# Node stage of a graph kernel: the stores of the per-block sums leave SyncE's queue and are issued by ScalarE, each behind its own copy

## Chip, cores and metric

The kernel runs on one core of one Trainium2 chip. The metric is the device time of one launch in microseconds (us); lower is better. Engine names: PE is TensorE, PEld its weight loads, DVE is VectorE, ACT is ScalarE, POOL is GpSimd, SP is SyncE. SPq and ACTq are the instruction sequencers of SP and ACT where they issue DMAs.

## What is computed

The reference is one layer of a graph network with a residual. `x` is 50000 x 128 in fp32, and there are 12500 edges.

```python
h = jnp.maximum(_layernorm(x, axis=-1), 0.0)
xx = _resmlp(h, w1[0], b1[0], w2[0], b2[0], wout[0])     # for every node
xs, xp, xd = (_resmlp(h, ... [m])[dst] for m in (1, 2, 3))
s = xx + segment_sum(gs * xs, src, n)
p = segment_sum(gp * xp[:, None, :], src, n)
d = segment_sum(gd * xd[:, None, :], src, n)
y = s + (pa * pb).sum(-2) + (da * db).sum(-2)
out = x + _resmlp(y, w1[4], b1[4], w2[4], b2[4], wout[4])
```

`_resmlp(x)` is `silu(x + silu(silu(x) @ w1 + b1) @ w2 + b2) @ wout`. `gs`, `gp`, `gd` come from the edge attributes; `pa`, `pb`, `da`, `db` are the halves of `p` and `d` times two matrices.

## The kernel before

The launch has three stages, and each of the five engines runs its own list of instructions through all of them; semaphores tie the lists together. The node stage (`first_stage`) ends some 410 us into the span, the edge stage (`edge_phase`) at about 880 us, and the final stage (`final_stage`) is the rest. The change lies in the node stage alone.

The nodes are cut into NB = 98 blocks of 512 rows; a block is a 128 x 512 tile, 256 KB. The node stage does two things at once. It normalises every block into `h` and stores it to the table `node_h` (`htab`), and for the first NA = 90 blocks it runs MLP 0 to the end and stores the result to `node_sums` (`ysum`). Beside this the edges are sorted in two passes by DVE (`picked`), PE (L859) and POOL's scatters (L506); POOL's `keep_pace` ties the scatters to PE's progress.

The work is pipelined by a counter k, written out by hand without a loop on the chip. In step k PE does four things in this order:

- the transpose of block k (L871), which waits for the normalised block from ACT (`nrm_a`) and DVE (`nrm_v`)
- the first matmul of block k-1 (L884), which waits for ACT's silu `s1`
- the second matmul of block k-2 (L891), which waits for `s2`
- the third of block k-3 (L899, into the bank `BANK_O`), which waits for `s3` and, by `row_done`, for the copy that empties that bank.

In two steps of five the seven bf16 matmuls of the sort (L859) stand between L871 and L884.

In step k ACT does, in this order:

- silu `s1` of block k (L798)
- part of the normalisation of block k+1 (L784; in most steps two tiles of 128 x 128, in some four, with DVE doing the rest at L626 and L635), one of them here and one behind L808
- silu `s2` of block k-1 (L808)
- silu `s3` of block k-2 (L817)
- the copy of block k-3 from the bank to `rowout` (L823), which raises `row_done`.

`rowout` has four slots, so the copy of block b also waits until the store of block b-4 has landed (`stored`). The copy is the last thing of a step.

SP's list in step k is: store of `h` of block k (`store_h`, L410), store of the sums of block k-4 (`store`, L400, which waits for `row_done`), load of the rows of block k+18 (`load_x`, L392; `xin` has 20 slots). Steps 12 to 19 also store zeros (L460). SP runs strictly in this order.

In the final stage ACT issues the stores of the output already (L1103), but there the row is made by DVE (L1054), and the store belongs to the block of four steps back.

Of the kernel before, what the change touches and what calls it, by code (L numbers as in the profile page):

```python
# [78 lines left out]
def gnn_kernel(nc, x, src, dst, attr3, attr32, attr5, w_rs, w_rp, w_rd, w_pp, w_pd,  # L79
# [15 lines left out]
    NB = -(-N // BLOCK)  # L95
    ND = 8
    FILL = 4
    NA = NB - ND
# [35 lines left out]
    with ctx:  # L134
# [48 lines left out]
        rowout = sb("rowout", [P, 4, TB, F])  # L183
# [51 lines left out]
        at = P * T  # L235
# [39 lines left out]
        def at(b):  # L275
            return slice(N - BLOCK, N) if b == NB - 1 else slice(b * BLOCK, (b + 1) * BLOCK)

        def first_stage():
# [106 lines left out]
            def sync(sp):  # L385
                def load_x(b):
                    s = b % NX
                    if b >= NX:
                        if by_vector(b - NX + 1):
                            sp.wait_ge(nrm_v, by_vector(b - NX + 1))  # L390
                        sp.wait_ge(nrm_a, b - NX + 1)
                    sp.dma_start(xin[:, s, :, :], xb_view(at(b), x)).then_inc(x_in[s], 16)  # L392

                def store(b):
                    s = b % 4
                    sp.wait_ge(row_done, b + 1)
                    if b == NB - 1:

                        sp.wait_ge(stored[(b - 1) % 4], 16 * ((b - 1) // 4 + 1))
                    sp.dma_start(xb_view(at(b), ysum), rowout[:, s, :, :]).then_inc(stored[s], 16)  # L400

                def store_h(b):
                    s = b % 4
                    sp.wait_ge(nrm_a, b + 1)
                    if by_scalar(b) < TB:
                        sp.wait_ge(nrm_v, by_vector(b + 1))
                    if b == NB - 1:

                        sp.wait_ge(h_stored[(b - 1) % 4], 16 * ((b - 1) // 4 + 1))
                    sp.dma_start(xb_view(at(b), htab), xn[:, s, :, :]).then_inc(h_stored[s], 16)  # L410

                load_x(0)
                load_x(1)
                sp.wait_ge(s_staged, 1)
                assert load_parts(src, st_src[:, :], sp, s_src, 1) == N_SRC
                load_x(2)
                load_x(3)
                sp.dma_start(w1_sb[:, m, :], w1[m, :, :]).then_inc(s_w, 16)
                with nc.allow_non_contiguous_dma(reason="biases to partitions"):
                    sp.dma_start(b1_sb[:, :], b1.rearrange("m k -> k m"), allow_slow_non_contiguous=True).then_inc(s_w, 16)  # L420
                    sp.dma_start(b2_sb[:, :], b2.rearrange("m k -> k m"), allow_slow_non_contiguous=True).then_inc(s_w, 16)
                sp.dma_start(w2_sb[:, m, :], w2[m, :, :]).then_inc(s_w, 16)
                sp.dma_start(wo_sb[:, m, :], wout[m, :, :]).then_inc(s_w, 16)
                for b in range(4, 8):
                    load_x(b)
                sp.wait_ge(s_staged, 2)
                n_rest = 0
                for dram, tile, per in ((dst, st_dst, 1), (attr3, st3, NP3), (attr5, st5, ND5), (attr32, st32, NRBF)):
                    flat = tile[:, :] if per == 1 else tile[:, :, :].rearrange("p t c -> p (t c)")
                    n_rest += load_parts(dram, flat, sp, s_edges, per)  # L430
                assert n_rest == N_REST
                for b in range(8, NX):
                    load_x(b)
                store_h(0)
                store_h(1)
                for k in range(2, NB + 4):
                    if k < NB:
                        store_h(k)
                    if k == 6:
                        sp.wait_ge(s_cst, 5)  # L440
                        sp.dma_start(w1_sb[:, m + 1:, :], w1[m + 1:, :, :].rearrange("m k n -> k m n")).then_inc(s_w2, 16)
                        sp.dma_start(w2_sb[:, m + 1:, :], w2[m + 1:, :, :].rearrange("m k n -> k m n")).then_inc(s_w2, 16)
                        sp.dma_start(wo_sb[:, m + 1:, :], wout[m + 1:, :, :].rearrange("m k n -> k m n")).then_inc(s_w2, 16)
                        sp.dma_start(wpp_sb[:, :], w_pp).then_inc(s_w2, 16)
                        sp.dma_start(wpd_sb[:, :], w_pd).then_inc(s_w2, 16)
                        for j in range(TB):
                            for n, w in enumerate((w_rp, w_rd, w_rs)):
                                sp.dma_start(wr_sb[j * Q:j * Q + NRBF, n, :], w).then_inc(s_w2, 16)
                    if k == 10:
                        for row, parts, each in groups:  # L450
                            sp.dma_start(by_src[row:row + parts * each, :].rearrange("(p t) w -> p t w", t=each),
                                         padrow[0:parts, 0:each, :]).then_inc(s_init, 16)
                        for lo in range(0, SPARE, TB):
                            n = min(TB, SPARE - lo)
                            sp.dma_start(ysum[N + lo * P:N + (lo + n) * P, :].rearrange("(t p) f -> p t f", p=P),
                                         zeros[:, 0:n * F].rearrange("p (t f) -> p t f", t=n)).then_inc(s_init, 16)
                    if 12 <= k < 12 + ND:
                        lo = (NA + k - 12) * BLOCK
                        hi = min(lo + BLOCK, N)
                        sp.dma_start(ysum[lo:hi, :].rearrange("(p t) f -> p t f", t=TB),  # L460
                                     zeros[0:(hi - lo) // TB, :].rearrange("p (t f) -> p t f", t=TB)).then_inc(s_init, 16)
                    if 0 <= k - 4 < NA:
                        store(k - 4)
                    if NX <= k + NX - 2 < NB:
                        load_x(k + NX - 2)
                for s in s_scat:
                    sp.wait_ge(s, 2 * 16 * CHUNKS)
                sp.wait_ge(s_init, 16 * (-(-SPARE // TB) + len(groups) + ND))
                with nc.allow_non_contiguous_dma(reason="one word of each row"):
                    for g in (0, 1):  # L470
                        load_group(sp, by_src, er, rq, nxt, g, g, TB, T, rows_in[g], rows_in[g] if g else first_index_in)
# [301 lines left out]
            def scalar(act):  # L773
# [19 lines left out]
                for k in range(NB + 3):  # L793
                    if k < NK:
                        act.wait_ge(xT_done, k + 1)
                        if k >= 3:
                            act.wait_ge(a_done, k - 2)
                        nc.scalar.activation(s1[:, k % 3, :], BANK_X[k % 4][:, :], ACT.Silu).then_inc(s1_done, 1)  # L798
                    norm(k + 1, 0)
                    norm(k + 1, 1)  # L800
                    norm(k + 1, 2)
                    if 0 <= k - 1 < NK:
                        act.wait_ge(a_done, k)
                        if k == 1:
                            act.wait_ge(s_w, 16 * 5)
                        if k >= 4:
                            act.wait_ge(b_done, k - 3)
                        nc.scalar.activation(s2[:, (k - 1) % 3, :], BANK_A[:, :], ACT.Silu, bias=b1_sb[:, m:m + 1]).then_inc(s2_done, 1)  # L808
                    norm(k + 1, 3)
                    if 0 <= k - 2 < NK:  # L810
                        act.wait_ge(b_done, k - 1)
                        if k - 2 >= NA:
                            act.wait_ge(nrm_v, by_vector(NB - NB % NX + 4 + FILL))
                        elif k >= 5:
                            act.wait_ge(o_done, k - 4)
                        target = s3[:, (k - 2) % 3, :] if k - 2 < NA else kept_rows(k - 2 - NA)
                        nc.scalar.activation(target, BANK_X[(k - 2) % 4][:, :], ACT.Silu, bias=b2_sb[:, m:m + 1]).then_inc(s3_done, 1)  # L817
                    if 0 <= k - 3 < NA:
                        b = k - 3
                        act.wait_ge(o_done, b + 1)  # L820
                        if b >= 4:
                            act.wait_ge(stored[b % 4], 16 * (b // 4))
                        nc.scalar.copy(rowout[:, b % 4, :, :].rearrange("p t f -> p (t f)"), BANK_O[:, :]).then_inc(row_done, 1)  # L823

            def tensor(pe):
                start = dict(stop=True, skip_group_check=True)
# [1191 lines left out]
```

## Time and profile before

| what | value |
|---|---|
| median of 3 runs | 1187.74 us (1185.68 to 1198.05) |
| the profiled execution's own time | 1187.62 us |
| its span, first to last instruction | 1185.8 us |
| around the span | 1.8 us |
| busy over the span: PE, DVE, ACT, POOL | 92%, 58%, 62%, 40% |
| mean granted TensorE clock | 0.977 of full |

"Span" is the time from the first to the last instruction of the profiled execution; its own time is that plus the 1.8 us around it. "Busy" counts an engine's own work. Register, branch, semaphore and DMA-issuing instructions are not counted as busy, so SP has no busy time at all, and what ACT spends on issuing a DMA does not show in ACT's share either. In a timeline the bracket behind a row tells how long the engine was idle before it and what ended that.

### The profile page before, as it was taken

To read this page: it belongs to the slowest core of one execution; us is meant where nothing else is said; L and a number is where in the kernel's file an instruction comes from. 1 tells how busy PE (TensorE), PEld (TensorE's weight loads), DVE (VectorE), ACT (ScalarE), POOL (GpSimd) and SP (SyncE) were. 2 spreads that over 40 slices of the span, in tenths; PEclk is the share of its full clock that TensorE was granted. 3 is DMA by queue.
4 is the path that set the end of the run, shared out by engine and by line. 5 is a ranking of instruction groups with operands and counts; after the bars stand their busy time and mean duration, and the time that the engine had idled before them with its cause. 6 is when DMAs were issued, how large, how long until landed. Compare 5 with 4: busy or idle time off the path is not lost.

```text
span 1185.8 us, 22908 instructions
## 1 busy us (share of the span) xinstructions
PE 1088.6 (92%) x6267; PEld 711.7 (60%) x6267; DVE 688.9 (58%) x2413; ACT 736.6 (62%) x1379; POOL 471.7 (40%) x433
## 2 busy tenths in 40 slices
PE   4978998987898659999999999999979999999998
PEld 2645665765666326666666666666736666666665
DVE  8976776766666226656665665655633444444432
ACT  4656878966778635665565565555536666666664
POOL 2355666155666442556556656655440000000000
PEclk9988999999999879999999999999999999999999
DMA  9667767855674443665556555555549999999984
GB/s 267 208 201 232 225 223 222 296 170 175 224 228 155 142 94 75 115 118 107 97 102 107 99 95 106 101 96 92 101 69 240 282 268 274 274 271 273 269 275 142
DMA packets 319187, 210.81 MB, mean 178 GB/s; under 512 B 204084, under 2 KB 240830, under 8 KB 318963
## 3 DMA queue, kind: packets, MB, share of 16 engines
q1 hardware_dynamic: 280770, 164.67, 50.7%
q0 software_dynamic: 24208, 19.29, 10.3%
q10 hardware_dynamic: 14112, 25.70, 6.2%
q8 instruction: 44, 0.72, 0.3%
q14 instruction: 53, 0.43, 0.1%
HBM read 107.15 MB, written 102.42 MB: 177 GB/s over the span
## 4 chain that ended last, share of the span: by engine, by line
PE 83%; DVE 6%; issue 5%; ACT 2%; another core or an unknown queue 2%; DMA 2%; POOL 0%; SPq 0%; ACTq 0%; POOLq 0%; DVEq 0%
PE quad L1133 8%; PE bank L1147 7%; PE bank L1769 6%; PE quad L884 5%; PE quad L1139 5%; PE bank L1779 5%; PE bank L899 5%; PE bank L1845 4%; PE quad L891 4%; PE bank L1815 4%; PE bank L1846 3%; PE quad L871 3%; PE quad L1855 2%; PE quad L1122 2%
## 5 line engine op out<-in xcount | busy, mean ns | idle before, releaser
L1421 POOL DMA_INDIRECT node_sums<-rowout,row_i x98 | 154.8, 1580 | 49.6 <-issue 28.7
L74 POOL DMA_INDIRECT yin<-node_h,er x98 | 99.2, 1012 | 165.1 <-DMA nxt<-edges_by_src 130.9
L1054 DVE TENSOR_TENSOR rowout<-bank,xin 128x512 f32<-128x512 f32 x98 | 67.8, 692 | 142.7 <-PE bank L1147 141.7
L1147 PEld LDWEIGHTS bank<-wo_sb,s 128*128 128x128 f32 x784 | 102.8, 191 | 47.8 <-issue 47.8
L899 PEld LDWEIGHTS bank<-wo_sb,s 128*128 128x128 f32 x720 | 95.3, 194 | 54.6 <-issue 54.5
L506 POOL DMA_INDIRECT edges_by_low<-pay,rank_i x98 | 99.7, 1017 | 69.5 <-issue 28.9
L1473 DVE SCALAR_TENSOR_TENSOR h<-bank,b_sb,hT 128x512 f32<-128x512 f32 (+1 forms) x75 | 55.5, 740 | 123.3 <-PE bank L1779 113.6
L506 POOL DMA_INDIRECT edges_by_src<-pay,rank_i x98 | 98.9, 1009 | 60.8 <-issue 24.4
L784 ACT ACTIVATE xn<-xin,nbias,rnorm 128x128 f32<-128x128 f32 x222 | 106.4, 493 | 13.0 <-DVE nbias L616 10.5
L681 DVE SCALAR_TENSOR_TENSOR picked<-bank,onehot 128x256 bf16<-128x256 f32 (+1 forms) x196 | 67.5, 387 | 74.1 <-PE bank L859 29.6
L1133 PE MATMUL quad<-s,w_sb 128*128 128x512 f32 x196 | 103.8, 612 | 0.8 <-ACT s L1071 0.7
L1147 PE MATMUL bank<-wo_sb,s 128*128 128x128 f32 x784 | 103.5, 275 | 0.9 <-DVE rowout L1054 0.9
L899 PE MATMUL bank<-wo_sb,s 128*128 128x128 f32 x720 | 96.9, 278 | 7.9 <-ACT rowout L823 5.7
L884 PE MATMUL quad<-s,w_sb 128*128 128x512 f32 x188 | 101.8, 625 | 0.1
L565 DVE BATCH_NORM_STATS2 stat<-xin 128x6 f32<-128x128 f32 x392 | 98.6, 283 | 1.1 <-DMA xin<-in_x_dram 1.1
L1652 ACT ACTIVATE s<-h 128x512 f32<-128x512 f32 (+1 forms) x75 | 46.6, 622 | 72.7 <-DVE h L1473 56.6
L1681 ACT COPY AB<-bank 128x512 f32<-128x512 f32 x98 | 58.1, 593 | 54.1 <-PE bank L1846 41.9
L1769 PE MATMUL bank<-s,w_sb 128*128 128x512 f32 (+1 forms) x150 | 79.9, 615 | 6.9 <-ACT s L1644 4.8
L871 PE MATMUL quad<-ident,xn 128*128 128x128 f32 x284 | 45.5, 284 | 38.7 <-issue 21.0
L808 ACT ACTIVATE s<-quad,b_sb 128x512 f32<-128x512 f32 x94 | 64.6, 687 | 21.4 <-PE quad L884 11.9
L1779 PE MATMUL bank<-s,w_sb 128*128 128x512 f32 (+1 forms) x150 | 76.2, 590 | 0.1
L891 PE MATMUL quad<-s,w_sb 128*128 128x512 f32 x142 | 75.7, 616 | 0.0
(208 smaller groups left out, 2254.4 us busy)
## 6 DMA issues: line engine op xcount, KB each, us to landing
xin<-in_x_dram SPq DMA_DIRECT2D x196, 256.0 KB
node_h<-xn SPq DMA_DIRECT2D x98, 256.0 KB
out_dram<-rowout ACTq DMA_DIRECT2D x98, 256.0 KB
node_sums<-rowout SPq DMA_DIRECT2D x90, 256.0 KB
yin<-node_sums SPq DMA_DIRECT2D x53, 256.0 KB, 3.7
yin<-node_sums SPq DMA_DIRECT2D x180, 64.0 KB, 3.2
src_in_every_row<-edge_src_row SPq DMA_DIRECT2D x24, 256.0 KB
border_sums_by_tile<-border_sums SPq DMA_DIRECT2D x24, 256.0 KB, 2.1
```

The source lines that it names most:

```text
L74: pool.indirect_dma_start(out=xg[:, s, j, :], out_offset=None, in_=x, in_offset=bass.IndirectOffsetOnAxis(ap=er[:, s, j, 1:2].bitcast(mybi ...
L506: nc.gpsimd.indirect_dma_start(out=ps.dram, out_offset=bass.IndirectOffsetOnAxis(ap=rank_i[:, t:t + 1], axis=0), in_=pay[:, t, :], in_offs ...
L565: last = nc.vector.bn_stats(stat[:, b % 32, j, :], xin[:, s, j, :])
L784: ins = nc.scalar.activation(xn[:, b % 4, j, :], xin[:, s, j, :], ACT.Relu, bias=nbias[:, q, i:i + 1], scale=rnorm[:, q, i:i + 1])
L884: nc.tensor.matmul(BANK_A[:, :], w1_sb[:, m, :], s1[:, (k - 1) % 3, :], start=True, stop=True).then_inc(a_done, 1)
L891: nc.tensor.matmul(BANK_X[(k - 2) % 4][:, :], w2_sb[:, m, :], s2[:, (k - 2) % 3, :], start=False, stop=True, skip_group_check=True).then_i ...
L899: last = nc.tensor.matmul(BANK_O[:, j * P:(j + 1) * P], s3[:, (k - 3) % 3, j * P:(j + 1) * P], wo_sb[:, m, :], start=True, stop=True)
L1133: nc.tensor.matmul(BANK_A[:, :], w1_sb[:, m, :], s1[:, s, :], start=True, stop=True).then_inc(a_done, 1)
L1147: last = nc.tensor.matmul(BANK_O[:, j * P:(j + 1) * P], s3[:, s, j * P:(j + 1) * P], wo_sb[:, m, :], start=True, stop=True)
L1421: nc.gpsimd.indirect_dma_start(out=ysum, out_offset=bass.IndirectOffsetOnAxis(ap=row_i[:, t % 2, j:j + 1], axis=0), in_=urow[:, t % 2, j, ...
L1769: nc.tensor.matmul(BANK_A[:, 0:e], w1_sb[:, MLP[m], :], s1[:, k % 2, 0:e], start=True, stop=True).then_inc(a_done, 1)
L1779: nc.tensor.matmul(BANK_B[:, 0:e], w2_sb[:, MLP[m], :], s2[:, m, 0:e], start=True, stop=True).then_inc(b_done, 1)
```

## The change

The store of a block's sums is taken out of SP's list. ACT issues it directly behind its copy of the same block, after a wait on `row_done` for that copy's own end. SP keeps the stores of `h`, the zeros and the loads. Everything else is the same; the branch for the last block falls away, since block NB-1 was never among the NA blocks stored here.

```diff
@@ def sync(sp) @@
-                def store(b):
-                    s = b % 4
-                    sp.wait_ge(row_done, b + 1)
-                    if b == NB - 1:
-
-                        sp.wait_ge(stored[(b - 1) % 4], 16 * ((b - 1) // 4 + 1))
-                    sp.dma_start(xb_view(at(b), ysum), rowout[:, s, :, :]).then_inc(stored[s], 16)
@@
-                    if 0 <= k - 4 < NA:
-                        store(k - 4)
                     if NX <= k + NX - 2 < NB:
                         load_x(k + NX - 2)
@@ def scalar(act) @@
                         nc.scalar.copy(rowout[:, b % 4, :, :].rearrange("p t f -> p (t f)"), BANK_O[:, :]).then_inc(row_done, 1)
+                        act.wait_ge(row_done, b + 1)
+                        act.dma_start(xb_view(at(b), ysum), rowout[:, b % 4, :, :]).then_inc(stored[b % 4], 16)
```

ACT's list of the kernel before, from the copy at the end of one step through the next step (a step with two normalisation tiles), with the semaphores that each row waits for; `rowout` is the tile that is stored, `xn` the normalised block, `s` the silus:

```order
L823 COPY rowout<-bank 128x512 [waits n_o_done]
L798 ACTIVATE s<-quad 128x512 [waits n_a_done,n_xT_done]
L784 ACTIVATE xn<-xin,nbias,rnorm 128x128 [waits h_stored3,n_xT_done,n_norm_steps_done]
L808 ACTIVATE s<-quad,b_sb 128x512 [waits n_b_done,n_a_done]
L784 ACTIVATE xn<-xin,nbias,rnorm 128x128 [waits n_xT_done,n_norm_steps_done]
L817 ACTIVATE s<-quad,b_sb 128x512 [waits n_o_done,n_b_done]
```

The changed kernel's list there, beginning with the rest of that step; all lines of ACT stand ten lower, L813 is the copy:

```order
L774 ACTIVATE xn<-xin,nbias,rnorm 128x128 [waits h_stored3,n_xT_done,n_norm_steps_done]
L798 ACTIVATE s<-quad,b_sb 128x512 [waits n_b_done,n_a_done]
L774 ACTIVATE xn<-xin,nbias,rnorm 128x128 [waits n_xT_done,n_norm_steps_done]
L807 ACTIVATE s<-quad,b_sb 128x512 [waits n_o_done,n_b_done]
L813 COPY rowout<-bank 128x512 [waits n_o_done]
L815 DMA node_sums<-rowout 128x512 [waits n_row_done]
L788 ACTIVATE s<-bank 128x512 [waits n_a_done,n_xT_done]
L774 ACTIVATE xn<-xin,nbias,rnorm 128x128 [waits h_stored0,n_xT_done,n_norm_steps_done]
```

One row came in, L815, between the copy and the next step's first silu. It waits for `n_row_done`, which the copy just ahead of it raises. There are 90 such rows.

SP's list of the kernel before, around the last store of zeros (`node_h` is the table of `h`, `node_sums` the sums, `xin` the rows of `x`):

```order
L410 DMA node_h<-xn 128x512 [waits n_rectified_by_vector,n_rectified_by_scalar]
L460 DMA node_sums<-zeros 84x512
L400 DMA node_sums<-rowout 128x512 [waits n_row_done]
L392 DMA xin<-in_x_dram 128x512 [waits n_rectified_by_scalar,n_rectified_by_vector]
L410 DMA node_h<-xn 128x512 [waits n_rectified_by_vector,n_rectified_by_scalar]
L400 DMA node_sums<-rowout 128x512 [waits n_row_done]
```

The changed kernel's list at the same place:

```order
L402 DMA node_h<-xn 128x512 [waits n_rectified_by_vector,n_rectified_by_scalar]
L452 DMA node_sums<-zeros 84x512
L392 DMA xin<-in_x_dram 128x512 [waits n_rectified_by_scalar,n_rectified_by_vector]
L402 DMA node_h<-xn 128x512 [waits n_rectified_by_vector,n_rectified_by_scalar]
L392 DMA xin<-in_x_dram 128x512 [waits n_rectified_by_scalar,n_rectified_by_vector]
```

The row L400 with its wait is gone, 90 times, and the load of `x` follows the store of `h` directly.

## Rows read from the trace of the kernel before

**Rows 1.** Busy time by stretch of the node stage; x is the number of instructions.

```profile
core 0: us, PE busy (x) PEld busy (x) DVE busy (x) ACT busy (x) POOL busy (x), PEclk, DMA share, GB/s
60.00:120.00 60.00, 48.62 (x229) 32.29 (x228) 40.61 (x240) 37.37 (x73) 32.82 (x33) 0.86 0.66 216
...
180.00:240.00 60.00, 56.84 (x334) 39.54 (x332) 43.30 (x221) 51.02 (x105) 23.19 (x24) 1.00 0.76 258
...
sum 368.00, PE 323.46 PEld 221.38 DVE 254.82 ACT 274.71 POOL 207.63; mean PE 46.21 PEld 31.63 DVE 36.40 ACT 39.24 POOL 29.66
```

**Rows 2.** Chain of waits, 34 to 402 us, shares by line.

```profile
by line: PE quad L884 16.5%; PE bank L899 16.3%; PE quad L891 12.3%; issue 10.9%; PE quad L871 7.7%; DVE picked L681 4.5%; another core or an unknown queue 4.5%; PE bank L859 4.3%; PE bank L891 3.5%; DVE stat L565 3.5%; PE bank L834 3.3%; P
```

**Rows 3.** Timeline, 157 to 165 us: start us, us, engine, line, operation.

```profile
156.73 0.61 PE L871 MATMUL bank<-ident,xn 128*128 128x128 f32 x4
...
157.09 0.58 ACT L823 COPY rowout<-bank 128x512 f32<-128x512 f32 x1
157.55 0.61 ACT L798 ACTIVATE s<-bank 128x512 f32<-128x512 f32 x1
157.69 0.34 SPq L400 DMA_DIRECT2D node_sums<-rowout  x1
...
158.99 0.51 ACT L784 ACTIVATE xn<-xin,nbias,rnorm 128x128 f32<-128x128 f32 x1
159.38 0.71 ACT L817 ACTIVATE s<-quad,b_sb 128x512 f32<-128x512 f32 x1
...
159.79 0.60 PE L871 MATMUL quad<-ident,xn 128*128 128x128 f32 x4
...
162.02 0.58 ACT L823 COPY rowout<-bank 128x512 f32<-128x512 f32 x1 [1.94 <-remote]
162.17 0.42 DVE L681 SCALAR_TENSOR_TENSOR picked<-bank,onehot 128x256 bf16<-128x256 f32 x1 [0.95 <-PE bank L859]
...
163.95 0.49 ACT L784 ACTIVATE xn<-xin,nbias,rnorm 128x128 f32<-128x128 f32 x1
...
164.54 0.63 PE L871 MATMUL quad<-ident,xn 128*128 128x128 f32 x4 [0.66 <-issue]
```

**Rows 4.** Timeline of ACT: first and last copy with a short step behind it.

```profile
40.90 0.58 ACT L823 COPY rowout<-bank 128x512 f32<-128x512 f32 x1 [0.42 <-PE bank L899]
...
398.73 0.59 ACT L823 COPY rowout<-bank 128x512 f32<-128x512 f32 x1
...
401.64 0.58 ACT L823 COPY rowout<-bank 128x512 f32<-128x512 f32 x1
```

**Rows 5.** Waits on PE and DVE, 34 to 402 us: us in total, times, longest.

```profile
PE quad L871 <- issue: 21.0, 24, 2.4
PE bank L871 <- issue: 13.0, 6, 3.9
...
DVE xn L626 <- DMA node_h<-xn: 13.1, 7, 2.5
```

**Rows 6.** ACT's copy L823 in the whole run: durations, and waits before it.

```profile
L823 ACT COPY rowout<-bank x90: 567/585/601, 33.9 to 401.6; 128x512 f32<-128x512 f32 x90
...
  remote: 22.0, 12
```

**Rows 7.** Waits of SP's queue, 34 to 402 us: us in total, times, longest.

```profile
SPq L410 <- ACT xn L784: 88.6, 57, 4.4
SPq L400 <- ACT rowout L823: 39.1, 31, 5.3
```

**Rows 8.** Stores issued by ACT in the final stage, and one of them in the timeline.

```profile
L1103 ACTq DMA_DIRECT2D out_dram<-rowout x98: 338/344/1093, 899.4 to 1183.3; - x98
...
1006.52 0.36 ACTq L1103 DMA_DIRECT2D out_dram<-rowout  x1
1006.54 0.62 ACT L1088 ACTIVATE s<-xn 128x512 f32<-128x512 f32 x1
1007.06 0.59 ACT L1071 ACTIVATE s<-quad 128x512 f32<-128x512 f32 x1
```

## The prediction, made before the changed kernel ran

> **What bounds the kernel now.** I read the node stage alone, since no instruction of the two later stages moves, and began with busy time by stretch. Over the 368 us from the first copy to the last, PE works 323.5 us and ACT 274.7 us; in the densest stretch, 180 to 240 us, PE is at 57 of 60 and ACT at 51 of 60 [rows 1]. So PE sets the pace, and ACT is close behind. The chain of waits says the same: the largest shares are PE's matmuls L884, L899 and L891, and 10.9% stands under "issue", where the profile names nobody [rows 2].
>
> The timeline tells who that nobody is. At 164.54 us PE begins the transpose L871 after 0.66 us of idle time put down to "issue". ACT's last normalisation tile began at 163.95 and took 0.49, so it ended at 164.44, and PE started 0.10 us behind it [rows 3]. L871 does wait for that tile. There are 30 such waits before L871 in the stage, 34.0 us together [rows 5], and in 29 steps of 89 PE starts L871 after an idle time of over 0.3 us just 0.10 us behind the end of an ACT tile. At those places PE stands still until ACT has come through its list. In that list the copy L823 is ahead of the silu and the tiles.
>
> The rhythm: a copy at 157.09, the next silu already at 157.55, while the copy still runs until 157.67. The engine takes the next instruction 0.46 us after the start of the copy [rows 3]. With nothing in its way ACT needs 2.9 us from copy to copy (398.73 to 401.64) [rows 4]; PE needs 3.06 (L871 at 156.73 and at 159.79) [rows 3], and some 0.8 more in the two steps of five that hold the sort's matmuls. On the average a step takes 367.7 / 89 = 4.13 us, as there are stalls besides.
>
> **What the change removes.** SP loses 90 issues of 0.34 us and the wait for the copy, 39.1 us in 31 pieces [rows 7]. Behind that wait stood the load of `x` for 18 blocks further on, and then the store of the next `h`. In the ACT and PE waits of this stretch no load of `x` is named. The store of `h` waits for ACT's tiles anyway (88.6 us in 57 waits [rows 7]), and those come after the copy in ACT's order. I cost the removal at 0. If that is wrong, it is a gain; see the rivals.
>
> **What it adds.** 90 times ACT now holds its list until its own copy is done, and then issues a DMA. No row of before shows this pair on ACT, so I put it together:
>
> - the copy runs to its end: 0.585 us (median of 90) [rows 6]
> - the semaphore: the copy at 157.09 ended at 157.67, and SP's store began at 157.69, so 0.02 [rows 3]
> - the issue: ACT's own stores in the final stage take 0.34 [rows 8]
> - until the next instruction starts: PE follows ACT by 0.10 at 164.54 [rows 3]; I take 0.10.
>
> Sum 1.05 us from the start of the copy to the next silu, in place of 0.46: 0.59, rounded to **0.6 us per block**. The low end is 0.48, with nothing between the issue and the silu. The high end is 0.69: in the final stage a silu starts at 1007.06, 0.18 us after an issue that ran from 1006.52 to 1006.88 [rows 8], so 0.58 + 0.02 + 0.36 + 0.18 = 1.14 to 1.15, less 0.46. That row shows too why stores cost ACT nothing today: L1088 starts at 1006.54, while the issue runs. There the sequencer has sent the silu ahead and issues beside it. Here it can't, since the wait is for the instruction just sent.
>
> The Trainium skill (DMA: Bandwidth & Descriptors, Issuing engines are not separate DMA queues) says that issuing from several engines saves only sequencer time, which is usually small beside the transfer. By that rule SP saves 90 issues that nobody waits for, and the sum is not changed by a faster transfer.
>
> **How much of 90 x 0.6 = 54 us reaches the end.** ACT has 368.0 - 274.7 = 93.3 us of idle time in the stretch [rows 1], so both ends are open: all hidden, or all paid. I went through ACT's timeline from copy to copy. In 33 of the 89 steps ACT idles less than 0.3 us, in 8 more less than 0.6; the first of these 41 follows the copy at 40.90, the last the one at 398.73 [rows 4]. In the other 48 it waits 0.6 us or more for PE, and the addition hides there. Summing 0.6 less the idle time over the 41 gives 19.8 us (15.1 with 0.48, 23.6 with 0.69).
>
> That takes each lag of ACT as a lag of PE. In a step with no idle time PE has a little room: the tile at 158.99 ends at 159.50, and L871 starts at 159.79 [rows 3], 0.29 us later, so 0.19 to 0.3 may slip. If ACT may always lag 0.3 us before PE feels it, and the lag is carried from step to step and worked off in idle time, the same list gives 13.1 us (8.5 with 0.48, 16.6 with 0.69). But behind a stall there is no room: at 162.02 to 164.54 ACT has no idle time and PE waits for it. I take **15 us**, nearer to 13.1, since most short steps don't follow each other.
>
> After the last copy, at 401.64, nothing is added. The lag stays to the end, because the scatters keep PE's pace and the edge stage begins when both are done. Sum, against the profiled execution's own 1187.62 us: 1187.6 + 15 = 1202.6. The median of the runs, 1187.74, is the same within 0.1 us, so the forecast for the median is **1202.7 us**, 1.3% slower. Its own range runs from 8.5 to 23.6 us, 1196 to 1211.
>
> **Rivals.**
>
> *No difference.* ACT may lag further than I think before PE feels it. The copy only has to be done before the next L899, the last matmul of PE's step, and the silus are each wanted later than the tiles. With room for 1.2 us the list gives 2.9 us, 1190.6. Against it stand the 29 starts of L871 right behind an ACT tile.
>
> *Faster.* Before the copy stand 22.0 us in 12 waits put down to "remote" [rows 6]; the copy also waits for the landing of the store four blocks back, which shares SP's queue with 256 KB loads and 256 KB stores of `h`. DVE waits 13.1 us for the landing of `h` in 7 cases [rows 5]. If these are landings held up in SP's queue, a second queue shortens them. All of the 22.0 less the 15 that ACT pays would be 1187.6 - 7 = 1180.6; with ACT's cost hidden too, 1165.6. Against it: at 162.02 the copy is released, and at 162.17 DVE's `picked`, which waits for PE and for no store [rows 3]; so both were held by PE. In its favour is a rule of the Trainium skill (the same page, Queues, rings and completion order): each DMA engine goes round its queues packet by packet, so that a store in a queue of its own would not wait behind loads. Worked out from this kernel's rows that is the case just priced, at 1180.6, and no row before shows a store overtaking. As DVE runs ahead of ACT by design (it centres block k+1 in step k), I give its 13.1 us no worth.
>
> *Much slower.* The longer ACT step can cost PE more than the sum says, if nothing is worked off in the idle time: the stalls are waits in a ring ACT to PE to ACT, and then each of the 90 additions is paid. That is 54 us, 1241.6. It decides if the 48 long steps each become longer by 0.6. PE's clock may join: in 60 to 120 us, with PE busy 48.6 of 60, it was granted 0.86 [rows 1].
>
> **How the numbers follow.** The forecast (ACT's lag paid in the short steps, 8.5 to 24 us): 0.66. No difference, below 8.5 us: 0.22. Faster: 0.06. Much slower, 24 us and more: 0.06. A measurement of this kernel tells about 1%, 11.9 us, from no change. Within the forecast about four parts in five lie above 11.9 us, 0.53, and with the much slower case that makes 0.59 for slower by over 1%. The rest of the forecast, 0.13, with the 0.22 and a part 0.01 of the faster case makes 0.36 within 1%, and 0.05 is faster by over 1%. The range for 8 in 10 takes in the forecast's own and most of the case of no difference: 1189 to 1213.
>
> **What the changed profile would show.** ACTq issues of `node_sums`, 90 of 0.34 us, each within 0.05 us of the end of a copy, and the silu behind them 1.05 us after the start of the copy in place of 0.46. The shortest copy to copy at 3.5 us in place of 2.9. ACT's busy time unchanged, and the last copy at about 417 us in place of 401.6. More idle time before L871 on PE than 34 us. SP's wait on the copy gone and no other in its place. The later stages as long as before. I would be wrong if the silu followed the copy in 0.5 us (the issue is hidden after all), if the last copy came at 402 (all absorbed), or if the "remote" waits before the copy went away, for then they were landings.

## The result, and the profile after

The change made the kernel slower by 0.69%. Over 20 runs of each the median is 1197.62 us (1190.12 to 1204.13) against 1188.95 us (1182.84 to 1198.05) before; the ratio is 1.0069, 95% interval 1.0049 to 1.0088, which is 8.2 us (5.8 to 10.5) on 1188.95. (The two medians themselves lie 8.7 us apart.) By the bound of about 1% that the prediction names, that is within what counts as "same"; the interval leaves no doubt about the sign. The profiled execution has a span of 1196.9 us, 11.1 more than before.

The busy time of the changed kernel, for the same stretches and with the same columns as [rows 1]:

```profile
60.00:120.00 60.00, 47.16 (x233) 31.32 (x234) 42.26 (x248) 38.03 (x75) 32.94 (x34) 0.94 0.69 216
...
180.00:240.00 60.00, 54.95 (x308) 37.33 (x307) 44.02 (x225) 49.35 (x101) 23.65 (x26) 1.00 0.78 251
...
sum 368.00, PE 319.78 PEld 217.16 DVE 252.83 ACT 272.46 POOL 201.71; mean PE 45.68 PEld 31.02 DVE 36.12 ACT 38.92 POOL 28.82
```

The loss shows in the densest stretch: PE does 308 matmuls in 180 to 240 us where it did 334, and works 55.0 us instead of 56.8. ACT, too, has less busy time there. Over the whole 368 us PE works 319.8 us instead of 323.5. An engine that is held back by its own list does not look busier; it does less in the same time.

ACT's timeline of the changed kernel, which answers to [rows 3]:

```profile
150.73 0.58 ACT L813 COPY rowout<-bank 128x512 f32<-128x512 f32 x1 [1.43 <-remote]
151.35 0.34 ACTq L815 DMA_DIRECT2D node_sums<-rowout  x1
151.79 0.60 ACT L788 ACTIVATE s<-quad 128x512 f32<-128x512 f32 x1 [0.47 <-ACT rowout L813]
...
153.62 0.68 ACT L807 ACTIVATE s<-bank,b_sb 128x512 f32<-128x512 f32 x1
154.19 0.58 ACT L813 COPY rowout<-bank 128x512 f32<-128x512 f32 x1
```

The silu starts 1.06 us after the start of the copy; it was 0.46 to 0.48. The bracket says that ACT was idle for 0.47 us before the silu and puts that down to ACT's own copy. The copy ended before these 0.47 us began, at 151.31 us; the issue, which does not count as busy, fills 0.34 of them. From copy to copy the step takes 3.46 us, where ACT's shortest was 2.9 [rows 4]. 39 of the 89 steps now take 3.44 to 3.46 us, and none is shorter.

The copy in the whole run of the changed kernel, to be read beside [rows 6]; the waits of PE from 34 to 415 us and of SP's queue from 34 to 409 us, the last copy, beside [rows 5] and [rows 7]; and the stores of the final stage, beside [rows 8]:

```profile
L813 ACT COPY rowout<-bank x90: 568/585/591, 34.3 to 408.7; 128x512 f32<-128x512 f32 x90
...
  remote: 23.8, 13
...
  ACT s L788: 19.3, 41
```

```profile
PE quad L863 <- issue: 23.1, 43, 2.4
...
PE bank L891 <- ACT rowout L813: 10.3, 5, 4.5
PE bank L863 <- issue: 10.2, 14, 3.0
```

```profile
SPq L402 <- ACT xn L774: 105.8, 33, 7.4
```

```profile
L1095 ACTq DMA_DIRECT2D out_dram<-rowout x98: 338/354/393, 910.5 to 1194.4; - x98
```

The copies span 408.7 - 34.3 = 374.4 us against 367.7, so 6.7 of the 11.1 us by which this execution is longer lie between the first and the last copy. Another 0.4 us lie before the first copy, and 4.0 between the last copy and the first store of the final stage (910.5 - 408.7 against 899.4 - 401.6). The final stage's stores take 283.9 us in both. The transpose L863 (L871 before) has 57 waits put down to "issue", 33.3 us in all, instead of 30 with 34.0: more waits, each shorter. The wait of 39.1 us in SP's queue for the copy is gone, but SP now waits 105.8 us for ACT's tiles instead of 88.6 [rows 7]: 17 of the 39.1 us came back as another wait. With what is gone nothing was won.

### The profile page after: what moved, and what is told of

Read it like the earlier page. It is cut to its first block, busy times and chain, and to the rows that moved or that the text cites. A ratio compares the mean times of both kernels' runs of the same rounds, so it can differ in the third digit from the quotient of the medians.

```text
span 1196.9 us, 22908 instructions
## 1 busy us (share of the span) xinstructions
PE 1091.1 (91%) x6267; PEld 710.7 (59%) x6267; DVE 689.4 (58%) x2413; ACT 738.0 (62%) x1379; POOL 468.6 (39%) x433
## 3 DMA queue, kind: packets, MB, share of 16 engines
q10 hardware_dynamic: 27072, 49.30, 11.2%
## 4 chain that ended last, share of the span: by engine, by line
PE 80%; issue 6%; ACT 5%; DVE 3%; another core or an unknown queue 2%; DMA 2%; ACTq 1%; SPq 0%; POOL 0%; POOLq 0%; DVEq 0%
PE quad L1125 8%; PE bank L1139 7%; PE bank L1761 6%; PE quad L1131 5%; PE bank L1771 5%; PE bank L891 5%; PE quad L876 5%; PE bank L1837 4%; PE bank L1807 4%; PE bank L1838 4%; PE quad L883 3%; PE quad L863 2%; PE quad L1846 2%; ACT xn L774 2%
## 5 line engine op out<-in xcount | busy, mean ns | idle before, releaser
L891 PEld LDWEIGHTS bank<-wo_sb,s 128*128 128x128 f32 x720 | 95.5, 195 | 56.9 <-issue 54.6
L891 PE MATMUL bank<-wo_sb,s 128*128 128x128 f32 x720 | 97.6, 279 | 11.5 <-ACT rowout L813 10.3
L1125 PE MATMUL quad<-s,w_sb 128*128 128x512 f32 x196 | 103.8, 611 | 0.7 <-ACT s L1063 0.7
L876 PE MATMUL quad<-s,w_sb 128*128 128x512 f32 x188 | 99.2, 610 | 0.8 <-ACT s L798 0.8
L863 PE MATMUL quad<-ident,xn 128*128 128x128 f32 x284 | 45.7, 285 | 43.2 <-issue 23.1
L1131 PE MATMUL quad<-s,w_sb 128*128 128x512 f32 x148 | 76.3, 598 | 0.0
L883 PE MATMUL quad<-s,w_sb 128*128 128x512 f32 x142 | 73.5, 600 | 0.0
```

Source lines behind the costliest of these rows:

```text
L876: nc.tensor.matmul(BANK_A[:, :], w1_sb[:, m, :], s1[:, (k - 1) % 3, :], start=True, stop=True).then_inc(a_done, 1)
L883: nc.tensor.matmul(BANK_X[(k - 2) % 4][:, :], w2_sb[:, m, :], s2[:, (k - 2) % 3, :], start=False, stop=True, skip_group_check=True).then_i ...
L891: last = nc.tensor.matmul(BANK_O[:, j * P:(j + 1) * P], s3[:, (k - 3) % 3, j * P:(j + 1) * P], wo_sb[:, m, :], start=True, stop=True)
L1125: nc.tensor.matmul(BANK_A[:, :], w1_sb[:, m, :], s1[:, s, :], start=True, stop=True).then_inc(a_done, 1)
L1131: nc.tensor.matmul(BANK_X[s][:, :], w2_sb[:, m, :], s2[:, s, :], start=in_squares(k, 2), stop=True, skip_group_check=True).then_inc(b_done, 1)
```

## The experiments

The theory of the prediction: the cost comes from ACT's list, held for 0.59 us behind each copy, less what ACT's idle time takes up. The rivals: it is the second queue; it is a landing that was late; or any wait in ACT's list is paid in full.

Each kernel was timed beside the kernel before on one chip. The chips of these experiments (three of them, here the second, third and fourth chip; the number of the first measurement's chip, here the first, is not recorded) ran the kernel before in 1116 to 1117 us and not in 1189. That turned out to be the most useful part, and the fifth experiment is about it. No experiment ran on a chip at 1189 us, so the cause is shown by experiment at 1117 us alone, and for the first measurement it rests on its two traces. In the diffs "..." stands for what is left out.

**Wait alone** (second chip; against the kernel before).

```diff
                         nc.scalar.copy(rowout[...], BANK_O[:, :]).then_inc(row_done, 1)
+                        act.wait_ge(row_done, b + 1)
```

Expected: 

> The kernel before, with one addition: behind its copy ACT waits for the copy's own end. The store stays in SP's list. Theory (the hold on ACT's list costs what the next silu is late, less what ACT's idle time and a lag of 0.3 to 0.6 us that PE does not feel take up): the silu starts about 0.7 us after the start of the copy instead of 0.46, so x = 0.25 us per block; the list of ACT's idle times of the kernel before gives +1.4 us with a free lag of 0.3 and +0.6 with 0.6, so a ratio of 1.000 to 1.002. Rival (the second queue and not the hold makes the change slow): ratio 1.000, and the same for the late store to be ten us slow. Rival (any wait in ACT's list is paid in full): 89 x 0.25 = 22 us, ratio 1.019.

Measured: 1116.08 us against 1116.71, ratio 0.9998 (0.9987 to 1.0009). ACT's timeline of this kernel:

```profile
150.69 0.58 ACT L823 COPY rowout<-bank 128x512 f32<-128x512 f32 x1
151.31 0.60 ACT L798 ACTIVATE s<-quad 128x512 f32<-128x512 f32 x1
...
152.75 0.69 ACT L808 ACTIVATE s<-quad,b_sb 128x512 f32<-128x512 f32 x1 [0.47 <-PE quad L885]
```

The silu starts 0.62 us after the copy's start, so the wait holds the list for 0.15 us, less than the 0.25 I had put down. It costs nothing: further down the list ACT still waits 0.47 us for PE. The rival that any wait is paid in full falls: 89 waits of 0.15 us would be 13 us.

**Store one step later** (second chip; against the changed kernel).

```diff
+                    if 0 <= k - 4 < NA:
+                        act.wait_ge(row_done, k - 3)
+                        act.dma_start(xb_view(at(k - 4), ysum), rowout[:, k % 4, :, :]).then_inc(stored[k % 4], 16)
                     if 0 <= k - 3 < NA:
...
-                        act.wait_ge(row_done, b + 1)
-                        act.dma_start(xb_view(at(b), ysum), rowout[:, b % 4, :, :]).then_inc(stored[b % 4], 16)
```

Expected: 

> The changed kernel, but ACT issues the store of a block one step later, behind the third silu and just ahead of the next copy, so that the wait for the copy's end is already over. Theory (hold): the issue lies beside the silu that is still running; next silu again 0.46 us after the start of the copy; 1188 to 1190 us, ratio to before 0.999 to 1.002. Rival (the queue of its own or the store's traffic on ACT's queue costs the time): stays at the changed kernel's 1.007. Rival (the second queue helps and the hold hides it): ratio under 0.998.

Measured: 1115.82 against 1116.71 us, ratio 0.9994 (0.9983 to 1.0006). It was run again on the fourth chip, where the kernel before took 1115.78 us. Expected: 

> The late store once more on the chip of this job. Theory: no hold, so ratio 0.998 to 1.002 on either kind of chip. Rival (where stalls are many, the second queue helps): under 0.998 on a chip at 1189.

Measured: ratio 1.0000 (0.9989 to 1.0011). ACT's timeline in this second run:

```profile
149.94 0.34 ACTq L810 DMA_DIRECT2D node_sums<-rowout  x1
...
150.82 0.59 ACT L816 COPY rowout<-bank 128x512 f32<-128x512 f32 x1
151.30 0.60 ACT L788 ACTIVATE s<-quad 128x512 f32<-128x512 f32 x1
```

All 90 stores are issued by ACT and travel on its queue, as in the changed kernel, and the silu follows the copy in 0.48 us. So neither ACT's issues nor the second queue cost or gain anything on these chips. On the fourth chip the changed kernel cost 21.1 us (below) and this one nothing: where the issue stands makes the difference.

**Store cut in two** (second chip; against the changed kernel).

```diff
-                            act.wait_ge(stored[b % 4], 16 * (b // 4))
+                            act.wait_ge(stored[b % 4], 32 * (b // 4))
...
-                        act.dma_start(xb_view(at(b), ysum), rowout[:, b % 4, :, :]).then_inc(stored[b % 4], 16)
+                        for h in (0, P // 2):
+                            act.dma_start(xb_view(at(b), ysum)[h:h + P // 2], rowout[h:h + P // 2, b % 4, :, :]).then_inc(stored[b % 4], 16)
```

Expected: 

> The changed kernel, with the store behind the copy cut into two DMAs of 64 partitions each, so ACT issues twice. Theory: x = 0.6 + about 0.4 = 1.0 us per block. The list of ACT's idle times gives +39 us without a free lag, +32 with 0.3, +27 with 0.6 and +20 with 1.2; after the changed kernel's +8 I expect +24 to +30 us, ratio 1.020 to 1.026. The growth is more than in proportion, since the idle time is used up. Rival (the loss comes from the queue or from a wait on PE that has nothing to do with ACT's list): ratio stays near 1.007. Rival (in proportion to the hold): 8 x 1.0 / 0.6 = 14 us, ratio 1.012.

Measured: 1203.47 us, ratio 1.0779 (1.0758 to 1.0800), 87 us slower. The direction was right, the size far off, and the trace says a part of why:

```profile
199.70 0.59 ACT L813 COPY rowout<-bank 128x512 f32<-128x512 f32 x1
200.32 1.12 ACTq L816 DMA_DIRECT2D node_sums<-rowout  x2
201.54 0.60 ACT L788 ACTIVATE s<-quad 128x512 f32<-128x512 f32 x1 [1.25 <-PE quad L877]
...
203.95 0.59 ACT L813 COPY rowout<-bank 128x512 f32<-128x512 f32 x1
```

The line of the issues in the whole run (shortest, median, longest in ns):

```profile
L816 ACTq DMA_DIRECT2D node_sums<-rowout x180: 473/588/1517, 34.4 to 425.3; - x180
```

The median of 588 ns is not the length of a usual issue. In the trace the first of each pair took 0.47 us and the second 0.62 (473 and 615 ns at 200.32), together 1.12 from start to end, where one issue over all 128 partitions takes 0.34. So the silu starts 1.84 us after the copy, a hold of 1.37 us and not 1.0, and the step takes 4.25 us. The other part is the chip: the 24 to 30 us had been worked out from a kernel at 1189 us. For a hold of 1.0 us the later sum (below) gives about 27 us at 1189 and about 50 at 1117.

**Store of zeros that waits for nothing** (second chip; against the kernel before).

```diff
-                    sp.wait_ge(row_done, b + 1)
...
-                    sp.dma_start(xb_view(at(b), ysum), rowout[:, s, :, :]).then_inc(stored[s], 16)
+                    sp.wait_ge(s_cst, 2)
+                    sp.dma_start(xb_view(at(b), ysum), zeros[:, :].rearrange("p (t f) -> p t f", t=TB)).then_inc(stored[s], 16)
...
-                        if b >= 4:
-                            act.wait_ge(stored[b % 4], 16 * (b // 4))
```

Expected: 

> The kernel before, but SP's store of the sums sends a tile of zeros and waits for no copy, and ACT's copy waits for no store. The term of the first MLP is left out of the result; every other instruction and all traffic stay. Theory (SP's wait for the copy and the landing of the stores cost nothing in before): ratio 0.998 to 1.002, and the waits put down to remote before the copy stay at about 22 us in 12 cases, since they are waits for PE. Rival (they are landings of stores in SP's queue): they go away, up to 22 us faster, ratio down to 0.981.

Measured: 1117.20 us, ratio 1.0012 (1.0002 to 1.0021). At 1117 us SP's wait for the copy and the copy's wait for the store's landing are worth nothing; there the removal costed at 0 was right. As for the "remote" waits this is inconclusive, because on this chip they don't occur at all:

```profile
L818 ACT COPY rowout<-bank x90: 569/585/587, 33.9 to 341.0; 128x512 f32<-128x512 f32 x90
...
  PE bank L894: 1.1, 4
```

Only the changed kernel's first profile speaks to it: there the stores had a queue of their own, and the "remote" waits stayed, 23.8 us in 13 (before 22.0 in 12).

**The changed kernel where the rest does not stall** (third chip). Expected: 

> The changed kernel once more, unaltered, beside the kernel before on the chip of this job. In the first four experiments the kernel before took 1117 us and not 1189, and its node stage shows hardly any stall: 55 of 89 steps of the zeros-store kernel take 3.0 us from copy to copy, ACT idles 31 us in 307. Theory (the cost is the hold of 0.59 us less ACT's idle time): with so little idle time nearly all of it shows. The same sum over that list gives +33 us without a free lag, +31 with 0.3, +29 with 0.6, so 1144 to 1150 us, ratio 1.025 to 1.030, if this chip too runs the kernel before in 1117; if it runs it in 1189, ratio 1.005 to 1.009. Rival (the cost of the change is fixed, 8 us, whatever the stalls): ratio 1.007 at 1117.

Measured: 1135.87 against 1116.42 us, ratio 1.0174 (1.0152 to 1.0197), 19.4 us. That is under the 1.025 to 1.030 expected from ACT's gaps, and far over the fixed 1.007. The same kernel once more, on the fourth chip. Expected: 

> The changed kernel unaltered, a third time, on whatever chip this job gets. Theory: the cost is the sum over the 89 steps of what the kernel before lacks to 3.47 us from copy to copy (2.88 us, ACT's shortest, plus 0.59), less a lag of about 0.3 us that is free. That gives 18 us where the kernel before runs in 1117 us (ratio 1.015 to 1.018) and 5 to 10 us where it runs in 1189 (1.004 to 1.009). Rival (a fixed cost): the same microseconds on both.

Measured: 1136.89 against 1115.78 us, ratio 1.0189 (1.0174 to 1.0205), 21.1 us, a little over the 1.015 to 1.018 expected. The cost is not fixed: 8 us beside a kernel of 1189, 19 to 21 beside the same kernel at 1117. To see the difference I profiled the kernel before on the third chip. Expected: 

> The kernel before, unaltered, for its trace on this chip. Theory (this chip has no stalls in the node stage where the one of the first traces had them): last copy at 341 us instead of 402, no waits put down to remote before the copy, PE busy 60 of 60 us from 60 to 180. Rival (what made 72 us lies in the later stages): last copy at 402.

Measured: 1117.06 us. Its busy time and its copies:

```profile
60.00:120.00 60.00, 60.00 (x338) 42.23 (x337) 58.20 (x338) 54.01 (x108) 45.76 (x46) 1.00 0.92 307
120.00:180.00 60.00, 60.00 (x331) 42.07 (x330) 48.59 (x250) 56.47 (x113) 44.71 (x44) 1.00 0.82 260
```

```profile
L823 ACT COPY rowout<-bank x90: 570/586/590, 34.0 to 341.3; 128x512 f32<-128x512 f32 x90
```

The same views of the changed kernel on this chip, and what PE's transpose waits for between its copies (34 to 362 us; the kernel before has no such wait from 34 to 342):

```profile
60.00:120.00 60.00, 58.55 (x321) 40.43 (x320) 54.34 (x314) 51.49 (x102) 43.95 (x45) 1.00 0.91 283
120.00:180.00 60.00, 58.18 (x309) 39.49 (x308) 46.59 (x245) 51.40 (x103) 42.26 (x42) 1.00 0.78 238
```

```profile
L813 ACT COPY rowout<-bank x90: 567/586/590, 33.4 to 361.8; 128x512 f32<-128x512 f32 x90
```

```profile
PE quad L863 <- issue: 4.7, 20, 0.5
PE bank L863 <- issue: 1.6, 7, 0.2
```

This pair is the clearest of all. The copies span 328.4 us instead of 307.3, which is 21.1 us more, and the two profiled executions differ by 21.0: the whole cost lies between the first and the last copy. From 60 to 180 us PE does 630 matmuls where it did 669.

In the kernel before PE is busy 60.0 of 60 us where it was busy 48.6 in [rows 1], and its granted clock there is 1.00 instead of 0.86; the last copy comes at 341.3 us instead of 401.6. Of the 72 us between the two medians 60 lie between the copies. Here 54 of the 89 steps take 3.04 to 3.05 us. The stalls of the first chip, which ended for ACT, DVE and POOL within 0.3 us (162.02 and 162.17 in [rows 3], and 162.27 for POOL), are missing.

In these traces I saw how the sum ought to be made. A step from the kernel before on the third chip:

```profile
154.68 0.59 ACT L823 COPY rowout<-bank 128x512 f32<-128x512 f32 x1
...
156.99 0.69 ACT L817 ACTIVATE s<-quad,b_sb 128x512 f32<-128x512 f32 x1
157.72 0.59 ACT L823 COPY rowout<-bank 128x512 f32<-128x512 f32 x1
```

It takes 3.04 us, and no row of ACT in it has a bracket. Yet ACT could do it in 2.88: the copy starts 0.73 us after the silu ahead of it, where it needs only 0.57 (153.62 to 154.19 in the first timeline of this part). ACT's rows overlap when its input is there in time, and a lost overlap is no gap. The time free in a step is its length less 2.88 us, not the gaps between ACT's rows. Worked out so from the kernel before on either chip, with a lag of 0.3 us that costs nothing (steps with more normalisation tiles are set against their own shortest, 3.65 us), and with the hold as each trace shows it:

| hold, us | kernel before at | sum | measured |
|---|---|---|---|
| 0.59, the change | 1189 | 10.5 (4.6 with a free lag of 0.6) | 8.2 (5.8 to 10.5) |
| 0.59, the change | 1117 | 18.4 | 19.4 and 21.1 |
| 1.07, below | 1117 | 57.7 | 63.4 |
| 1.37, two halves | 1117 | 83.0 | 87.0 |

The sum was set up after the fifth experiment and the two halves, so the test of it in this table is what the fourth chip gave: 21.1 us and the row of 1.07. At 1117 us every measured value lies above its sum, by 1.0 to 5.7 us.

**One more issue** (fourth chip; against the changed kernel, with `stored` counted as for the two halves).

```diff
+                        act.dma_start(scratch[b * P:(b + 1) * P, :], rowout[:, b % 4, 0, 0:16]).then_inc(stored[b % 4], 16)
```

Expected: 

> The changed kernel with one more issue behind the store: ACT also writes 16 columns of the slot to a scratch table, 8 KB, so a second issue of about 0.34 us and no traffic worth a name. Theory: hold 1.0 us, 3.88 us from copy to copy at the least; the sum over the steps of the kernel before (distances, free lag 0.3) gives about 50 us at 1117 (ratio 1.040 to 1.048) and about 27 at 1189 (1.018 to 1.028). Rival (in proportion to the hold, from 19.5 us at 0.59): 33 us at 1117, 1.030.

Measured: 1179.40 us, ratio 1.0568 (1.0545 to 1.0590), 63.4 us.

```profile
200.51 0.59 ACT L814 COPY rowout<-bank 128x512 f32<-128x512 f32 x1
201.12 0.34 ACTq L816 DMA_DIRECT2D node_sums<-rowout  x1
201.50 0.45 ACTq L817 DMA_DIRECT2D extra_rows<-rowout  x1
202.05 0.60 ACT L789 ACTIVATE s<-quad 128x512 f32<-128x512 f32 x1 [0.95 <-PE quad L878]
...
204.45 0.59 ACT L814 COPY rowout<-bank 128x512 f32<-128x512 f32 x1
```

The extra issue took 0.45 us and not 0.34, so the hold is 1.07 and the step 3.94. In proportion to the 21.1 us at 0.59 on this chip that would be 38 us; it is 63. The sum with the hold of 1.0 had said about 50, with 1.07 it says 57.7. The trace shows something that the sum leaves out, from 34 to 404 us:

```profile
DVE xn L617 <- DMA node_h<-xn: 29.0, 12, 3.9
PE quad L865 <- DVE xn L626: 12.0, 15, 2.0
PE bank L865 <- DVE xn L626: 5.5, 6, 2.1
```

PE's transpose waits 21 times, 17.5 us in all, for DVE's part of the normalised block; in the kernel before on the third chip it did so twice, 2.9 us. DVE itself waits 29.0 us for landings of `h`, against 11.2 there. So with a long hold the delay seems to reach PE by a second way too, the later stores of `h` and DVE. How much of the missing 5.7 us that is was not tested. Note the bracket at 202.05: it blames PE's L878, though by PE's rows that had ended at 201.62 and ACT's queue was issuing until 201.95.

**Store behind the silu** (third chip; against the changed kernel).

```diff
                         nc.scalar.activation(s1[:, k % 3, :], BANK_X[k % 4][:, :], ACT.Silu).then_inc(s1_done, 1)
+                    if 0 <= k - 4 < NA:
+                        act.wait_ge(row_done, k - 3)
+                        act.dma_start(xb_view(at(k - 4), ysum), rowout[:, k % 4, :, :]).then_inc(stored[k % 4], 16)
```

The store behind the copy is taken out here too. Expected: 

> The changed kernel, but the store stands one instruction later in ACT's list, behind the first silu of the next step. The wait is for the same copy. Theory: the sequencer is held until 0.60 us after the start of the copy and issues until 0.95; the silu, sent ahead, runs from 0.46 to 1.06. So the tile behind it starts at 1.05 instead of 0.95, a hold of 0.1 us per block, and the list of the zeros-store kernel gives +0.2 to +3 us: ratio 1.000 to 1.003. Rival (each wait of ACT on its own result costs the time, wherever it stands): as e5, 1.025.

Measured: 1118.12 against 1116.42 us, ratio 1.0018 (1.0005 to 1.0032).

```profile
149.43 0.58 ACT L816 COPY rowout<-bank 128x512 f32<-128x512 f32 x1
149.91 0.60 ACT L788 ACTIVATE s<-quad 128x512 f32<-128x512 f32 x1
150.05 0.34 ACTq L791 DMA_DIRECT2D node_sums<-rowout  x1
150.51 0.49 ACT L774 ACTIVATE xn<-xin,nbias,rnorm 128x128 f32<-128x128 f32 x1
```

The same wait and the same issue, one instruction later, cost 2 us instead of 19 to 21. The issue now lies beside a silu that was sent ahead, and the tile behind it starts 0.60 us after that silu instead of 0.49. With the late store it shows that what costs is the place of the issue and not the issue or the wait. No version was faster than the kernel before by more than its interval.

## Why the prediction was right, and where it was off

*What bounds the kernel.* Right: PE sets the pace with ACT close behind, and a longer ACT list is passed on to PE at the transpose. The reading of "issue" before L871 as ACT's tile is borne out: each lengthening of the hold (0.59, 1.07, 1.37 us) lengthened the steps, and on the third chip 27 such waits appear where there were none.

*What is removed costs 0.* Right at 1117 us: the store of zeros without any wait and the late store are both within 0.12% of the kernel before. On a chip at 1189 us it was not tested.

*0.59 us per block.* Right: 1.06 us from copy to silu, predicted 1.05, and its parts are in the row: copy 0.58, issue 0.34 starting 0.04 behind it, 0.10 until the silu. The rule of the Trainium skill (DMA: Bandwidth & Descriptors, Issuing engines are not separate DMA queues) that a second issuing engine saves only sequencer time agrees with these runs: with 90 issues off SP's sequencer the late store took 0.9994 and 1.0000 of the kernel before.

*How much reaches the end.* This is the term that was mis-sized: 15 us predicted, 8.2 (5.8 to 10.5) measured. The step that failed is "Summing 0.6 less the idle time over the 41". Gaps between ACT's rows understate its room, as the step of 3.04 us above shows. By the distance from copy to copy less 2.88 us there are 37 steps, and the sum is 17.2 instead of 19.8, and 10.5 instead of 13.1 with the lag of 0.3. I had then gone up from 13.1 to 15 for places where PE has no room; that was the wrong way. These two corrections explain 4.5 of the 6.8 us; the rest lies within the interval, or asks for a free lag between 0.3 and 0.6. At 1117 us the measured values ask for a lag under 0.3, so no one lag fits both, and what sets it stays open. The range held, but within it the chances leaned the wrong way: 0.59 stood on slower by over 1%, 0.36 on within 1%, which is what came.

*The rivals.* "No difference" was nearer than its 0.22 says: by the ratio the cost is 8.2 us, just under its bound of 8.5, by the two medians 8.7, just above. "Faster" and "much slower" did not come on the first chip. Whether the "remote" waits are landings is not settled by an experiment; that they stayed with the queues apart speaks against it. But the prediction's own argument, that copy and `picked` "were held by PE" at 162 us, does not follow from the rows of PE in that step (kernel before, first chip):

```profile
158.90 1.05 PE L899 MATMUL bank<-wo_sb,s 128*128 128x128 f32 x8
160.22 0.93 PE L859 MATMUL bank<-onehot,ident_h 128*128 128x256 bf16 x7
```

By these rows (whose ends the profile models) L899 ended at 159.95 and L859 at 161.15, and the copy and `picked`, which wait for them, began only at 162.02 and 162.17. What held them is open. PE's clock was not lower after the change (mean 0.982 against 0.977).

*The signs named in advance.* The issue's place, the silu's start and the shortest step (3.44, said 3.5) came as described. SP's wait on the copy is gone as said, but another grew in its place, that for ACT's tiles from 88.6 to 105.8 us. The last copy came at 408.7 us, not 417. The idle time before the transpose did not grow (33.3 us against 34.0); there are more and shorter waits there, and L891 waits 10.3 us for the copy in 5 waits. On this chip that sign failed, and on the third chip it came. That nothing is added after the last copy is not what this pair of executions shows, with 4.0 us more between the last copy and the first store of the final stage; that is less than the spread of single runs, and on the third chip all of the difference lies between the copies.

## What to carry to other kernels

In this kernel a DMA issue on a compute engine cost nothing or next to nothing (0 and 2 us for 90) when something sent ahead was still running beside it. When it waited for the very instruction before it, it held the engine's list for the rest of that instruction and its own full length, 0.59 us each time. Put the issue behind the next instruction or one step later. To tell how much an addition to an engine's list will cost, take for each step its length less the shortest that this engine ever needed, not the gaps; here that came out 1 to 6 us low at 1117 us, where the gaps came out 10 us high. And expect the cost to be larger where the rest stalls less: 19 to 21 us here, against 8.

## What was not expected of the hardware

The same kernel took 1189 us in the first measurement and 1116 to 1117 us later on three chips, 60 of the 72 us between the copies of the node stage. There ACT, DVE and POOL of the first took up work within 0.3 us of each other after being idle, as at 162.02, 162.17 and 162.27 us after 1.94, 0.95 and 1.25 us; on the third chip no such place is found between the copies. What those stalls are, and whether the chip or something else at the time of the first measurement made them, stays open: no experiment ran under the same conditions.

An issue over 128 partitions of 2048 bytes each took 0.34 us. Of two issues over 64 partitions each, one right behind the other, the first took 0.47 us and the second 0.62. An issue of 128 partitions by 64 bytes, right behind a full one, took 0.45. So cutting a store in two made the issues more than three times as long in all (1.12 us against 0.34).
